# Softmax attention in a fused macaron block: the sums of the exponentials behind k's projection, the value product's third and fourth quarter in one run

## The chip, the core and the metric

The kernel runs on one NeuronCore of one Trainium2 chip, in one launch. The metric is the device time of that launch in microseconds (us), lower is better. The core has five instruction streams that work side by side and meet at semaphores: TensorE (PE, matrix products into the PSUM banks; PEld is its weight load), VectorE (DVE), ScalarE (ACT), GpSimdE (POOL) and SyncE (SP), which here only issues DMAs. Each stream is in order: an instruction that waits holds back all that stands behind it on its engine.

## The reference, cut to what matters

Eight sequences of 512 tokens with 128 channels pass six layers: a quantised feed-forward layer, softmax attention, the feed-forward layer again, a mixture of experts, a linear attention of depth 6, the mixture of experts again. The change lies in the softmax attention, with 16 heads of 64 channels, computed in float32:

```python
q = split_heads(x @ Wq.T); k = split_heads(x @ Wk.T); v = split_heads(x @ Wv.T)
sim = jnp.einsum('bhid,bhjd->bhij', q, k) * scale
m = jnp.max(sim, axis=-1, keepdims=True); e = jnp.exp(sim - m)
attn = e / (jnp.sum(e, axis=-1, keepdims=True) + EPS)
out = jnp.einsum('bhij,bhjd->bhid', attn, v)
return out.transpose(0, 2, 1, 3).reshape(B, N, INNER) @ Wo.T + bo
```

## The kernel before

The attention stage works on pairs of heads: 8 sequences x 8 pairs are 64 pairs, numbered g. It is one software pipeline, written out by hand as one loop per engine over periods (here called turns) g = -2 to 66. There is no scheduler: the order of the calls in each engine's loop is the order of its instructions, and semaphores tie the loops together. What concerns one pair is spread over four turns. In turn g, the engines do the following (kt = 0 to 3 are the four quarters of 128 keys, and TensorE's loop body goes through them):

- TensorE, in each quarter: `scores_turned(g, kt)` and `less_maximum(g, kt)` (lines 1269 and 1276, the scores with keys on the partitions, less the maximum), then `scores(g + 1, kt)` (line 1248, the scores of the next pair, from which only the maxima are taken). After quarter 0 it adds q's projection of pair g + 2 and the output product of pair g - 3 (lines 1297, 1337). After quarter 1: `add_up(g - 1)` (line 1314: sums of the exponentials, four products that fill four strips of bank `sums`), and `values(g - 1, 0)`, `values(g - 1, 1)` (line 1324: exponentials times v, in float32, into the single bank `pv`). After quarter 2: k's projection of pair g + 2 and `values(g - 1, 2)`. After quarter 3: `values(g - 1, 3)`, v's projection (line 1302) and `max_turned(g + 1)` (line 1257, which turns the maxima; it shares the bank `sums`).
- ScalarE takes the exponentials of pair g (line 1166, two for each quarter), the rounded high parts of q and k of pair g + 2 (`high`, line 1152), and copies the sums of pair g - 1 to SBUF (`total_out`, line 1172).
- VectorE takes the row maxima (`neg_max`, line 1073, two reductions for each quarter), the low parts of q and k (`low`, line 1089), the diagonal of maxima (`max_rows`, line 1081), the reciprocal of the sums (`invert`, line 1096), and the division `normalise(g - 2)` (line 1103), which empties `pv`.
- GpSimdE adds the four quarters of exponentials (line 1002) and makes the low part of the output (line 989).
- SyncE spreads the reciprocals of a pair from 32 partitions per head and half over the 64 partitions of that head, with eight DMAs (line 980), after `invert` and after the `normalise` before, since both use the one tile `rinv`.

The waits that tie a pair to the next are these. `normalise(g - 2)` waits for all eight DMAs of its pair. `values(g - 1, 0)`, the first product into `pv`, waits for `normalise(g - 2)`. `scores(g + 1, kt)` waits for the maxima of the quarter before it. `max_turned(g + 1)` waits for all maxima of pair g + 1 and for `total_out(g - 1)`. `add_up(g - 1)` waits for GpSimdE's sums, for the `total_out` before and for `max_rows(g + 1)`.

Every eighth turn `add_x` (lines 1109 and 1113) adds a sequence's output to x on VectorE, and from turn 28 on `early` puts small pieces of the next stage there. The bodies of the loops:

Of the kernel before, what the change touches and what calls it, by code (L numbers as in the profile page):

```python
# [912 lines left out]
def attn_stage(nc, mem, tag, splits=(), ahead=None):  # L913
# [7 lines left out]
    with ExitStack() as ctx:  # L921
# [42 lines left out]
        live = lambda g: 0 <= g < PAIRS_ALL  # L964
        PERIODS = range(-2, PAIRS_ALL + 3)

        with nc.Block() as block:
# [53 lines left out]
            def _(dve):  # L1021
# [70 lines left out]
                def invert(g):  # L1092
                    dve.wait_ge(total_done, g + 1)
                    if g:
                        dve.wait_ge(rinv_in, 16 * R_DMAS * g)
                    nc.vector.reciprocal(packed, total).then_inc(packed_done, 1)  # L1096
# [26 lines left out]
                for g in PERIODS:  # L1123
                    if live(g + 1):
                        neg_max(g + 1, 0)
                    if live(g - 2):
                        normalise(g - 2)
                    if live(g + 2):
                        low(g + 2, 0)
                    early(g)  # L1130
                    if live(g - 3) and (g - 3) % PAIRS == PAIRS - 1:
                        add_x((g - 3) // PAIRS)
                    if live(g + 1):
                        neg_max(g + 1, 1)
                    if live(g - 1):
                        invert(g - 1)
                    if live(g + 1):
                        neg_max(g + 1, 2)
                    if live(g + 2):
                        low(g + 2, 1)  # L1140
                    if live(g + 1):
                        neg_max(g + 1, 3)
                        max_rows(g + 1)

            @block.scalar
            def _(act):
                def high(g, which):
                    act.wait_ge(qk_done, 2 * g + 1 + which)
                    if g >= RING:
                        act.wait_ge(t_done, 8 * (g - RING + 1))  # L1150
                    scale = (DH ** -0.5 / W_ATTN, 1.0 / W_ATTN)[which]
                    nc.scalar.mul(high_of[which][g % RING][:], proj[:], scale).then_inc(hi_done, 1)

                def values_in(g):
                    act.wait_ge(v_done, g + 1)
                    if g >= 2:
                        act.wait_ge(pv_done, g - 1)
                    nc.scalar.mul(vv[g % 2][:].rearrange("p t d -> p (t d)"), proj[:], 1.0 / W_ATTN).then_inc(v_out, 1)

                def exp(g, kt):  # L1160
                    if kt == 0 and g >= 2:
                        act.wait_ge(pv_done, g - 1)
                        act.wait_ge(added, 2 * (g - 1))
                    for head in range(2):
                        act.wait_ge(t_done, 8 * g + 2 * kt + head + 1)
                        nc.scalar.activation(pT[g % 2][:, head, kt, :], turned[head][:], ACT.Exp).then_inc(exp_done, 1)  # L1166

                def total_out(g):
                    act.wait_ge(sums_done, g + 1)
                    if g:  # L1170
                        act.wait_ge(packed_done, g)
                    nc.scalar.activation(total, sums[:, 0:HALF], ACT.Copy, bias=SM_EPS).then_inc(total_done, 1)  # L1172

                def split(k, phase):
                    src, hi, lo, scale = splits[k]
                    if phase == 0:
                        if k == 0:
                            act.wait_ge(mem["moe_w_loaded"], 16 * 4)
                        nc.scalar.mul(src, src, scale).then_inc(w_scaled, 1)
                    else:  # L1180
                        act.wait_ge(w_scaled, k + 1)
                        nc.scalar.copy(hi, src).then_inc(w_hi, 1)

                def early(g):
                    b = EARLY_AT.get(g + 2)
                    if b is not None:
                        if b == 0:
                            act.wait_ge(early_known, 1)
                        else:
                            act.wait_ge(early_ratio_done, b)  # L1190
                        for t in range(TPB):
                            c = b * TPB + t
                            done = nc.scalar.activation(early_xn[:, t, :], mem["x"][:, c, :], ACT.Identity, bias=early_shift[:, c:c + 1])
                        done.then_inc(early_centred, 1)
                    b = EARLY_AT.get(g + 1)
                    if b is not None:
                        act.wait_ge(early_centred, b + 1)
                        for t in range(TPB):
                            c = b * TPB + t
                            done = nc.scalar.activation(early_xn[:, t, :], early_xn[:, t, :], ACT.Identity, scale=early_ln["rstd"][:, c:c + 1])  # L1200
                        done.then_inc(early_xn_done, 1)
                    b = EARLY_AT.get(g - 3)
                    if b is not None:
                        act.wait_ge(early_ratio_done, b + 1)
                        if b:
                            act.wait_ge(early_xg_done, b)
                        nc.scalar.activation(early_square[:], early_ratio, ACT.Square, scale=CURVE).then_inc(early_square_done, 1)

                def o_high(g):
                    act.wait_ge(o_done, g + 1)  # L1210
                    if g >= 2:
                        act.wait_ge(out_done, g - 1)
                    nc.scalar.copy(o16[g % 2][:, 0, :], oT[g % 2][:]).then_inc(o_hi, 1)

                for g in PERIODS:
                    if live(g):
                        exp(g, 0)
                    if live(g + 2):
                        high(g + 2, 0)
                    if live(g - 2):  # L1220
                        o_high(g - 2)
                    if live(g):
                        exp(g, 1)
                    if live(g - 1):
                        total_out(g - 1)
                    if 0 <= g < 2 * len(splits):
                        split(*divmod(g, 2))
                    early(g)
                    if live(g):
                        exp(g, 2)  # L1230
                    if live(g + 2):
                        high(g + 2, 1)
                    if live(g):
                        exp(g, 3)
                        values_in(g)

            @block.tensor
            def _(pe):
# [104 lines left out]
                for g in PERIODS:  # L1343
                    for kt in range(TPB):
                        if live(g):
                            scores_turned(g, kt)
                            if kt:
                                less_maximum(g, kt)
                        if live(g + 1):
                            scores(g + 1, kt)  # L1350
                        if kt == 0:
                            if live(g):
                                less_maximum(g, 0)
                            if live(g + 2):
                                project(g + 2, 0)
                            if live(g - 3):
                                output(g - 3)
                        elif kt == 1 and live(g - 1):
                            add_up(g - 1)
                            values(g - 1, 0)  # L1360
                            values(g - 1, 1)
                        elif kt == 2:
                            if live(g + 2):
                                project(g + 2, 1)
                            if live(g - 1):
                                values(g - 1, 2)
                        elif kt == 3:
                            if live(g - 1):
                                values(g - 1, 3)
                            if live(g):  # L1370
                                project(g, 2)
                            if live(g + 1):
                                max_turned(g + 1)
# [770 lines left out]
```

## Time and profile before

| What | Value |
|---|---|
| Runs | 1844.03, 1845.36, 1847.65 us; median 1845.36 |
| Profiled execution | 1844.77 us; its span 1842.6 us |
| PE busy | 1502.9 us (82%), PEld 843.7 us (46%) |
| DVE busy | 1384.0 us (75%) |
| POOL busy | 1100.4 us (60%) |
| ACT busy | 971.0 us (53%) |
| Granted TensorE clock | 0.905 of full speed over the span |

The span is the time from the first to the last instruction of one profiled execution, and all durations below are from it. Shares over the whole span mix nine stages with different limits. The attention stage runs from about 185 to 995 us of the span and is the longest; the page's line of fortieths shows PE at nine tenths all through it, at full clock. Its 64 pairs repeat one pattern, so a turn's length times 64 is nearly the stage.

The page's groups give the costs of one instruction in this stage: an exponential 594 ns (line 1166), a row maximum 684 ns (line 1073), the reciprocal 1743 ns (line 1096), an addition on POOL 1270 ns (line 1002), and a DMA of the reciprocals 1.8 us from issue to landing (line 980).

### The profile page before, as it was taken

The page shows a single profiled execution, that of the slowest core. Times are in us where ns is not written, and L with a number is a line of the kernel's source. Part 1 is how long each engine was busy: PE and PEld are TensorE (multiplying, and loading weights), DVE is VectorE, ACT ScalarE, POOL GpSimd, SP SyncE. Part 2 cuts the span into 40 slices and gives each one's busy share as a digit, 9 for nine tenths or more (in the row PEclk, how much of TensorE's full clock was granted, in tenths as well). Part 3 has the DMA queues.
Part 4 walks back from the last instruction along what each step waited for, and adds up shares of the span by engine and source line. Part 5 has one row for each costly group of instructions (what it writes and reads, how often), then busy time and mean ns, then how long its engine had stood idle before and what let it go on. Part 6 is the DMA issues. An engine that isn't in the chain of part 4 may idle for free. (4 is left out here: it accounts for less than half of the span.)

```text
span 1842.6 us, 32753 instructions
## 1 busy us (share of the span) xinstructions
PE 1502.9 (82%) x10611; PEld 843.7 (46%) x10611; DVE 1384.0 (75%) x2959; ACT 971.0 (53%) x2327; POOL 1100.4 (60%) x1434
## 2 busy tenths in 40 slices
PE   2776899999999999999996775069749999840896
PEld 1554233333333333333333555047438888740573
DVE  7997677778788878887773988358578888771683
ACT  2544466566555655555553543047328888620672
POOL 1231477877776767777773244747436666757473
PEclk9896899999999999999998887579879999955898
DMA  7000000000000000000000000233400000012335
GB/s 224 1 1 1 9 21 24 24 21 21 24 24 20 24 24 24 22 21 24 24 22 14 1 0 31 73 83 107 135 3 2 2 2 2 1 41 74 89 109 163
DMA packets 90181, 70.54 MB, mean 38 GB/s; under 512 B 16608, under 2 KB 84640, under 8 KB 90016
## 3 DMA queue, kind: packets, MB, share of 16 engines
q1 hardware_dynamic: 81312, 49.57, 10.0%
q0 software_dynamic: 8704, 18.89, 2.9%
q8 instruction: 89, 1.46, 0.3%
q14 instruction: 76, 0.62, 0.1%
HBM read 29.32 MB, written 22.30 MB: 28 GB/s over the span
## 5 line engine op out<-in xcount | busy, mean ns | idle before, releaser
L1166 ACT ACTIVATE at_pT<-at_turned 128x512 f32<-128x512 f32 x512 | 278.0, 594 | 262.4 <-PE at_turned L1276 262.4
L1073 DVE TENSOR_REDUCE at_nmax<-at_score 128x1 f32<-128x512 f32 x512 | 328.8, 684 | 111.2 <-PE at_score L1248 110.5
L1002 POOL TENSOR_TENSOR m_rows<-m_rows,at_pT 128x512 f32<-128x512 f32 x256 | 319.6, 1270 | 58.7 <-ACT at_pT L1166 58.7
L1324 PE MATMUL at_pv<-at_pT,at_v 128*64 128x512 f32 x1024 | 261.6, 611 | 0.9 <-DVE at_oT L1103 0.9
L1497 POOL DMA_INDIRECT by_token<-m_ysb,m_dest x144 | 137.9, 957 | 86.3 <-DVE m_ysb L1555 52.1
L1002 POOL TENSOR_TENSOR m_rows<-at_pT 128x512 f32<-128x512 f32 x128 | 159.7, 1267 | 46.6 <-ACT at_pT L1166 46.6
L989 POOL TENSOR_TENSOR at_o<-at_oT,at_o 128x512 f16<-128x512 f32 x64 | 77.1, 1205 | 150.3 <-issue 131.8
L1480 POOL DMA_INDIRECT by_expert<-m_rows,m_gate_slot x128 | 123.1, 962 | 60.5 <-issue 38.0
L639 POOL TENSOR_TENSOR f_hq<-f_hg,f_hsc 128x704 f32<-128x704 f32 x32 | 45.0, 1406 | 144.1 <-DVE f_hg L168 142.4
L1096 DVE RECIPROCAL m_rows<-m_rows 128x256 f32<-128x256 f32 x64 | 111.5, 1743 | 3.7 <-ACT m_rows L1172 3.6
L1297 PE MATMUL at_proj<-m_rows 128*128 128x512 f16 x384 | 108.3, 392 | 4.0 <-DVE at_own L1121 2.4
L1324 PEld LDWEIGHTS at_pv<-at_pT,at_v 128*64 128x64 f32 x1024 | 56.7, 135 | 118.2 <-issue 118.2
L1699 PE MATMUL m_x<-m_ident,m_xin 128*128 128x128 f32 x144 | 23.6, 290 | 106.2 <-DMA m_xin<-by_expert 106.2
L1710 PE MATMUL m_h<-m_w,m_x 128*128 x432 | 107.6, 386 | 3.0 <-DVE m_x L1532 3.0
L1269 PE MATMUL at_turned<-at_high_q,at_high_k 64*128 64x512 f16 x512 | 102.5, 388 | 1.0 <-ACT at_pT L1166 0.5
L1248 PE MATMUL at_score<-at_high_k,at_high_q 64*128 64x512 f16 x512 | 99.2, 381 | 3.0 <-DVE at_nmax L1073 2.3
L1269 PE MATMUL at_turned<-at_low_q,at_high_k 64*128 64x512 f16 x512 | 99.0, 378 | 0.0
L1269 PE MATMUL at_turned<-at_high_q,at_low_k 64*128 64x512 f16 x512 | 98.8, 377 | 0.0
L1276 PE MATMUL at_turned<-at_mdiag,at_unit 64*128 64x512 f16 x512 | 98.7, 377 | 0.0
L761 PE MATMUL f_gate<-m_wguT,f_xqT 128*128 128x352 f32 x128 | 63.5, 584 | 41.0 <-DVEq L570 39.5
L1269 PEld LDWEIGHTS at_turned<-at_high_q,at_high_k 64*128 64x128 f16 x512 | 25.2, 93 | 121.8 <-ACT at_pT L1166 56.6
L1636 ACT CAST m_x<-m_x 128x512 f16<-128x512 f32 x36 | 21.1, 586 | 112.7 <-PE m_x L1699 110.6
(384 smaller groups left out, 3727.4 us busy)
## 6 DMA issues: line engine op xcount, KB each, us to landing
m_rows<-m_rows SPq DMA_DIRECT2D x512, 32.0 KB, 1.8
m_xin<-by_expert SPq DMA_DIRECT2D x144, 72.0 KB
m_rows<-by_token SPq DMA_DIRECT2D x32, 256.0 KB, 4.8
by_token<-m_ysb,m_dest POOLq DMA_INDIRECT x144, 2.3
m_x<-in_x SPq DMA_DIRECT2D x8, 256.0 KB, 4.9
by_expert<-m_rows,m_gate_slot POOLq DMA_INDIRECT x128, 2.3
out_x<-m_x SPq DMA_DIRECT2D x8, 256.0 KB, 4.0
by_expert<-m_pad SPq DMA_DIRECT2D x18, 72.0 KB, 1.6
```

The lines of the kernel that those rows point to most:

```text
L1002: done = nc.gpsimd.tensor_tensor(acc, before, pT[g % 2][:, head, kt, :], ALU.add)
L1073: nc.vector.tensor_reduce(nmax[:, head * DH + qt:head * DH + qt + 1], score[head][:], AX.X, ALU.max, negate=True)\
L1096: nc.vector.reciprocal(packed, total).then_inc(packed_done, 1)
L1166: nc.scalar.activation(pT[g % 2][:, head, kt, :], turned[head][:], ACT.Exp).then_inc(exp_done, 1)
L1248: nc.tensor.matmul(score[head][:], high_of[0][g % RING][rows, qt * P:(qt + 1) * P], high_of[1][g % RING][rows, :], start=True, stop=True). ...
L1269: nc.tensor.matmul(turned[head][:], k_of[1][k][rows, tile], q_of[0][k][rows, :], start=(n == 0), stop=False)
L1276: nc.tensor.matmul(turned[head][:], unit[rows, :], mdiag[rows, :, :].rearrange("p t q -> p (t q)"), start=False, stop=True).then_inc(t_don ...
L1297: last = nc.tensor.matmul(proj[:], w[:, w_part, cols], x(x_part, 0, SEQ), start=(i == 0), stop=(i == 2))
L1324: last = nc.tensor.matmul(pv[halves[head], :], vv[g % 2][:, kt, halves[head]], pT[g % 2][:, head, kt, :], start=(kt == 0), stop=(kt == TPB ...
L1480: nc.gpsimd.indirect_dma_start(dram_rows, bass.IndirectOffsetOnAxis(slot[:, k, t:t + 1], 0), rows[k][:, t, :], None).then_inc(scattered, 16)
L1497: nc.gpsimd.indirect_dma_start(mem["dram_y_all"], bass.IndirectOffsetOnAxis(dest[j // TPB % DESTS][:, j % TPB:j % TPB + 1], 0), ysb[q % YS ...
L1710: last = nc.tensor.matmul(h[j % 3][:], x16[n % 2][:, x_part, tile], mem["w12_16"][:, w_part, ds(e, 1), :].rearrange("p e h -> p (e h)"), s ...
```

## The change

Nothing is computed otherwise. Four calls change their places. On TensorE, `add_up(g - 1)` goes from quarter 1 to quarter 2, behind k's projection, and `values(g - 1, 2)` from quarter 2 to quarter 3, in front of `values(g - 1, 3)`. On ScalarE, `total_out(g - 1)` goes behind the exponentials of quarter 2 and k's high part. On VectorE, `invert(g - 1)` goes behind the maxima of quarter 2 and k's low part.

```diff
 # VectorE
                     if live(g + 1):
                         neg_max(g + 1, 1)
-                    if live(g - 1):
-                        invert(g - 1)
                     if live(g + 1):
                         neg_max(g + 1, 2)
                     if live(g + 2):
                         low(g + 2, 1)
+                    if live(g - 1):
+                        invert(g - 1)
                     if live(g + 1):
                         neg_max(g + 1, 3)
                         max_rows(g + 1)
 # ScalarE
                         exp(g, 1)
-                    if live(g - 1):
-                        total_out(g - 1)
...
                         exp(g, 2)
                     if live(g + 2):
                         high(g + 2, 1)
+                    if live(g - 1):
+                        total_out(g - 1)
                     if live(g):
                         exp(g, 3)
 # TensorE
                         elif kt == 1 and live(g - 1):
-                            add_up(g - 1)
                             values(g - 1, 0)
                             values(g - 1, 1)
                         elif kt == 2:
                             if live(g + 2):
                                 project(g + 2, 1)
                             if live(g - 1):
-                                values(g - 1, 2)
+                                add_up(g - 1)
                         elif kt == 3:
                             if live(g - 1):
+                                values(g - 1, 2)
                                 values(g - 1, 3)
```

TensorE before, from the score pair that ends quarter 1 to the end of quarter 3, without the four products ahead of each later score pair (`at_sums<-m_rows` are the sums, `at_pv` the value product, `at_proj` with 128x512 k's projection and with 128x128 x12 v's):

```order
L1248 MATMUL at_score<-at_high_k,at_high_q 128x512 x2
L1314 MATMUL at_sums<-m_rows 32x256 x4
L1324 MATMUL at_pv<-at_pT,at_v 64x512 x4
...
L1248 MATMUL at_score<-at_high_k,at_high_q 128x512 x2
L1297 MATMUL at_proj<-m_rows 128x512 x3
L1324 MATMUL at_pv<-at_pT,at_v 64x512 x2
...
L1248 MATMUL at_score<-at_high_k,at_high_q 128x512 x2
L1324 MATMUL at_pv<-at_pT,at_v 64x512 x2
L1302 MATMUL at_proj<-m_rows 128x128 x12
L1257 MATMUL at_sums<-m_ident,at_nmax 128x128
```

The same quarters in the changed kernel:

```order
L1248 MATMUL at_score<-at_high_k,at_high_q 128x512 x2
L1324 MATMUL at_pv<-at_pT,at_v 64x512 x4
...
L1248 MATMUL at_score<-at_high_k,at_high_q 128x512 x2
L1297 MATMUL at_proj<-m_rows 128x512 x3
L1314 MATMUL at_sums<-m_rows 32x256 x4
...
L1248 MATMUL at_score<-at_high_k,at_high_q 128x512 x2
L1324 MATMUL at_pv<-at_pT,at_v 64x512 x4
L1302 MATMUL at_proj<-m_rows 128x128 x12
L1257 MATMUL at_sums<-m_ident,at_nmax 128x128
```

The value product stands in two runs of four instead of runs of four, two and two, and the sums come one quarter later.

VectorE before, one turn from the division to the diagonal of maxima:

```order
L1103 TENSOR_TENSOR at_oT<-at_pv,m_rows 128x512
L1089 SCALAR_TENSOR_TENSOR at_low_q<-at_proj,at_high_q 128x512
L1073 TENSOR_REDUCE at_nmax<-at_score 128x1 x2
L1096 RECIPROCAL m_rows<-m_rows 128x256
L1073 TENSOR_REDUCE at_nmax<-at_score 128x1 x2
L1089 SCALAR_TENSOR_TENSOR at_low_k<-at_proj,at_high_k 128x512
L1073 TENSOR_REDUCE at_nmax<-at_score 128x1 x2
L1081 TENSOR_TENSOR at_mdiag<-at_sums,at_own 128x512
```

The same turn in the changed kernel:

```order
L1103 TENSOR_TENSOR at_oT<-at_pv,m_rows 128x512
L1089 SCALAR_TENSOR_TENSOR at_low_q<-at_proj,at_high_q 128x512
L1073 TENSOR_REDUCE at_nmax<-at_score 128x1 x4
L1089 SCALAR_TENSOR_TENSOR at_low_k<-at_proj,at_high_k 128x512
L1096 RECIPROCAL m_rows<-m_rows 128x256
L1073 TENSOR_REDUCE at_nmax<-at_score 128x1 x2
L1081 TENSOR_TENSOR at_mdiag<-at_sums,at_own 128x512
```

The reciprocal stands behind one pair of maxima and k's low part more than before. SyncE's code is as it was: its eight DMAs follow the reciprocal, wherever that stands.

## Rows read from the trace of the kernel before

**Rows 1.** Busy time by stretch: length, PE, PEld, DVE, ACT, POOL, clock, DMA share, GB/s.

```profile
221.00:945.00 724.00, 723.66 (x5597) 271.18 (x5593) 579.02 (x838) 421.17 (x816) 536.97 (x437) 1.00 0.09 23
```

**Rows 2.** Timeline, TensorE, one turn: start, duration, engine, line, operation, count, idle before.

```profile
911.28 0.64 PE L1314 MATMUL at_sums<-m_rows 128*32 128x256 f32 x8
...
911.85 1.94 PE L1324 MATMUL at_pv<-at_pT,at_v 128*64 128x512 f32 x8
...
913.72 0.39 PE L1269 MATMUL at_turned<-at_high_q,at_high_k 64*128 64x512 f16 x2
...
914.59 0.38 PE L1248 MATMUL at_score<-at_high_k,at_high_q 64*128 64x512 f16 x2
...
914.90 0.82 PE L1297 MATMUL at_proj<-m_rows 128*128 128x512 f16 x3
...
915.66 1.08 PE L1324 MATMUL at_pv<-at_pT,at_v 128*64 128x512 f32 x4
...
916.67 0.39 PE L1269 MATMUL at_turned<-at_high_q,at_high_k 64*128 64x512 f16 x2
...
919.54 0.28 PE L1257 MATMUL at_sums<-m_ident,at_nmax 128*128 128x128 f32 x1
...
919.75 0.39 PE L1269 MATMUL at_turned<-at_high_q,at_high_k 64*128 64x512 f16 x2
```

**Rows 3.** Timeline, VectorE beside one score pair of TensorE, same turns.

```profile
900.32 1.74 DVE L1096 RECIPROCAL m_rows<-m_rows 128x256 f32<-128x256 f32 x1
...
902.33 0.38 PE L1248 MATMUL at_score<-at_high_k,at_high_q 64*128 64x512 f16 x2
...
904.13 0.69 DVE L1089 SCALAR_TENSOR_TENSOR at_low_k<-at_proj,at_high_k 128x512 f16<-128x512 f32 x1
...
909.84 0.68 DVE L1103 TENSOR_TENSOR at_oT<-at_pv,m_rows 128x512 f32<-128x512 f32 x1
...
912.58 1.27 DVE L1073 TENSOR_REDUCE at_nmax<-at_score 128x1 f32<-128x512 f32 x2
...
917.96 1.29 DVE L1073 TENSOR_REDUCE at_nmax<-at_score 128x1 f32<-128x512 f32 x2 [0.71 <-PE at_score L1248]
...
922.10 0.68 DVE L1103 TENSOR_TENSOR at_oT<-at_pv,m_rows 128x512 f32<-128x512 f32 x1
```

**Rows 4.** Timeline, end of the stage, waits for the copies.

```profile
958.90 0.68 DVE L1103 TENSOR_TENSOR at_oT<-at_pv,m_rows 128x512 f32<-128x512 f32 x1
...
969.56 0.69 DVE L1103 TENSOR_TENSOR at_oT<-at_pv,m_rows 128x512 f32<-128x512 f32 x1 [0.79 <-DMA m_rows<-m_rows]
...
972.73 1.75 DVE L1096 RECIPROCAL m_rows<-m_rows 128x256 f32<-128x256 f32 x1 [2.48 <-ACT m_rows L1172]
...
974.51 5.54 SPq L980 DMA_DIRECT2D m_rows<-m_rows  x8
...
981.37 0.69 DVE L1103 TENSOR_TENSOR at_oT<-at_pv,m_rows 128x512 f32<-128x512 f32 x1 [6.88 <-DMA m_rows<-m_rows]
...
982.21 3.65 PE L1324 MATMUL at_pv<-at_pT,at_v 128*64 128x512 f32 x16 [0.94 <-DVE at_oT L1103]
...
983.03 1.75 DVE L1096 RECIPROCAL m_rows<-m_rows 128x256 f32<-128x256 f32 x1 [0.97 <-ACT m_rows L1172]
...
991.06 0.69 DVE L1103 TENSOR_TENSOR at_oT<-at_pv,m_rows 128x512 f32<-128x512 f32 x1 [6.28 <-DMA m_rows<-m_rows]
```

**Rows 5.** Line 980, all copies of the stage: issue time in ns, min/median/max.

```profile
L980 SPq DMA_DIRECT2D m_rows<-m_rows x512: 507/591/1712, 214.7 to 989.2; - x171
```

**Rows 6.** Stretches of two other stages, and a wait in each (columns as above).

```profile
80.00:90.00 10.00, 7.96 (x39) 5.66 (x38) 9.58 (x16) 3.89 (x6) 2.45 (x2) 0.83 0.00 0
...
85.15 1.18 PE L761 MATMUL f_gate<-m_wguT,f_xqT 128*128 128x352 f32 x2 [1.85 <-DVEq L570]
...
1100.00:1116.00 16.00, 11.45 (x74) 9.18 (x73) 15.33 (x34) 6.57 (x10) 2.87 (x3) 1.00 0.00 1
...
1112.70 0.87 PE L785 MATMUL f_turn_h<-m_ident,f_hq 128*128 128x128 f32 x6 [1.81 <-POOL f_hq L639]
```

## The prediction

> **What bounds the kernel now.** I read the page first: the attention stage is the long stretch in which TensorE (PE) is busy nine tenths. Then the table of stretches for its steady part [rows 1]: PE is busy 723.66 of 724.00 us at full clock, VectorE (DVE) 579.02. So PE's stream sets the pace of a turn, and everything else has some slack. One turn's length is read from the same instruction twice: `normalise` starts at 909.84 and 922.10 [rows 3], so a turn is 12.27 us (12.26 by these two; the neighbours repeat 12.27), and there are 64.
>
> Next I looked for the slack of what the change moves. The reciprocal (`invert`) starts at 900.32, and the division that needs it after the eight DMAs starts at 909.84 [rows 3]: 9.52 us are there for it. How many are needed is seen only where DVE really waits for the DMAs, at the end of the stage [rows 4]: reciprocal at 972.73, division at 981.37 (8.64 us); reciprocal at 983.03, division at 991.06 (8.03 us). The parts: 1.75 for the reciprocal, the rest SyncE, which issues the eight one behind the other (median 0.59 us each [rows 5], the last one lands 1.8 us after its issue by the page). The 8.64 has one slow issue in it: the eight take 5.54 us [rows 4] instead of the some 4.9 that eight medians give, and slow ones reach 1.71 us [rows 5]. I take 8.2 on average, near the 8.03, since the median issue is the rule; bounds 8.03 and 8.64. So the slack in the kernel before is 9.52 - 8.2 = 1.3 us. That is the number on which this change turns.
>
> **The change part by part.**
>
> PE. A run of four quarter-head products of the value product takes 913.72 - 911.85 = 1.87 us, one of two takes 916.67 - 915.66 = 1.01 [rows 2]. Two runs of two become one of four: 2 x 1.01 - 1.87 = 0.15 us less per turn. The sums stand between other neighbours, but in as many changes of kind as before; I cost that at nothing (bounds -0.05 and +0.1: the dearest change in these rows is that from the value product, the cheapest under 0.05). If PE stayed the bound, a turn would be 12.12 us.
>
> ACT. `total_out` stands behind k's high part. The sums now start one k projection behind the score pair of quarter 2: 914.90 - 914.59 = 0.31, plus 915.66 - 914.90 = 0.76 [rows 2], 1.07 us. They take some 0.6 (911.85 - 911.28 = 0.57 [rows 2]), and ACT needs the time until k's high part is out in any case, since k's low part starts 904.13 - 902.33 = 1.80 us after that score pair [rows 3]. The copy (0.39) then lies beside k's low part (0.69) on DVE. Cost: nothing; if that cover were gone, some 0.2 us.
>
> DVE. Its order is now: maxima of quarter 2, k's low part, reciprocal, maxima of quarter 3. Measured from the score pair of quarter 2, the low part starts at 1.80 and the reciprocal 0.65 later (0.69 less a small overlap), at 2.45. Before, the reciprocal started 902.33 - 900.32 = 2.01 before that pair [rows 3]. The pair itself comes 0.57 earlier (the sums no longer stand ahead of it). So the reciprocal moves 2.01 + 2.45 - 0.57 = 3.9 us later in the turn. The slack was 1.3, and the turn is 0.15 shorter: the spread reciprocals come 3.9 - 1.3 + 0.15 = 2.7 us too late for `normalise`.
>
> What stands behind that wait: on DVE, q's low part and the maxima of quarter 1. On PE, `values(g - 1, 0)`, since `pv` is emptied by this division, and behind it everything. So the pace is no longer PE's stream but a ring of dependencies, once round per turn:
>
> - division starts, to first value product on PE: 982.21 - 981.37 = 0.84 [rows 4];
> - value run and four scores products, to the score pair of quarter 2: 914.59 - 911.85 = 2.74 [rows 2];
> - score pair to k's low part (exponentials and high part on ACT between them): 1.80 [rows 3];
> - low part to reciprocal: 0.65;
> - reciprocal to the next division: 8.2 (8.03 to 8.64).
>
> Sum 14.23 us (14.06 to 14.67), against 12.27: +1.96 per turn. PE alone would need 12.12, so it stands idle some 2 us in each turn, in one piece, in front of the first value product.
>
> Does the maxima's chain add to it? Reciprocal at 2.45, 1.7 for it, 1.29 for two maxima, under 0.1 to PE: `max_turned` at 5.5 after the score pair. PE would be there by 0.31 + 0.76 + 0.57 + 0.87 (scores products of quarter 3, 914.59 - 913.72) + 0.31 + 1.87 + 0.68 (v's projection, by 919.54 less the end of the run before) = 5.4 [rows 2]. It waits 0.1 us, but not on the ring: between `max_turned` and the idle piece PE has 2 us to spare. The 0.71 us that DVE waited ahead of those maxima [rows 3] is used up.
>
> Sum for the stage:
> - 60 full turns x 1.96 = 117.6;
> - the first division comes 3.9 later by its reciprocal and 9.52 - 8.2 = 1.3 sooner after it: +2.6;
> - the last three turns have no projections of later pairs. Before they took 991.06 - 958.90 = 32.2 [rows 4]. In the ring they lose k's low part and some of the matmuls, by an estimate 0.8, 1.0 and 2.2 us of 14.2: 38.6, so +6.4;
> - `add_x` stands between q's low part and the maxima of quarter 1. In such a turn these maxima start 912.58 - 909.84 = 2.74 after the division [rows 3] and end 1.3 later, at 4.05; the score pair of quarter 2 wants them at 0.84 + 2.74 = 3.58. +0.5 in 7 turns: +3.5. The `early` pieces are shorter (under 1 us) and hide;
> - TensorE's clock. Idle pieces of this size bring it down in some rows and not in others: in one stretch with a wait of 1.85 us the granted clock was 0.83 over 10 us, in another with waits up to 1.81 it stayed at 1.00 [rows 6]. One fall cost there (1 - 0.83) x 10 = 1.7 us of full-speed time. The ring's usual idle piece is near that edge (12.12 of 14.23 us busy: 2.1 less the short switches that are in both), and turns with a slow issue are over it. I put 8 falls: +13.6 (bounds 0 and 60 x 1.7 = 102).
>
> Together +144. On the profiled execution's 1844.8 us that gives 1988.5; the median of the runs shown, 1845.4, is 0.6 above it, so I forecast 1989.
>
> **A page weighed against the rows.** The rows show 6.3 to 6.9 us from the end of the reciprocal to the division [rows 4]. The Trainium skill, "DMA: Bandwidth & Descriptors", section "Anatomy of one DMA — SWDGE (gpsimd) path", gives a fixed cost of about 2.0 us per DMA, and its "Rules for kernel authors" say that issued early and waited for late, this fixed cost overlaps. Whoever costs the eight copies as one overlapped group by it has 1.75 + 2.0 = 3.75 us instead of 8.2, by an estimate, finds the division in time and forecasts the gain on PE alone. The trace disagrees in one point only: the landings overlap, the issues don't.
>
> **The rivals.**
>
> (1) The copies are in time after all, and the turn stays PE's. Mechanism: the turn's start slides enough, or the eight issues run closer than in [rows 4], so that the division isn't held. Then 0.15 x 62 = 9 us less: 1836. From which point: the reciprocal to the division has to take under 8.2 - 2.7 = 5.5 us. Against it: both waits measured are over 8, and the least issue is 0.507 us [rows 5], eight of which with reciprocal and landing still make 7.6. Chance 5%.
>
> (2) The copies are in time, but the reciprocal ahead of the maxima of quarter 3 holds `max_turned` back: 5.5 against 5.4, 0.1 per turn, which eats most of the 0.15. 1842 to 1846, no difference. Same evidence against it. Chance 3%.
>
> (3) The ring holds, and the clock falls in half of the turns or more. For it: the idle piece of some 2 us is longer than the 1.85 before which the clock fell [rows 6]. Against it: PE is busy without a break for 12 us in between, where in that stretch it wasn't (7.96 of 10 us). 30 falls give 1989 - 14 + 51 = 2026, 60 give 2077. Chance 20%. The Trainium skill, "TensorE: Matmul & The Clock Gate", section "HAM oscillation — how this bites in real kernels", tells of kernels in which each wait for a DMA lets the clock fall; by it this is the case to fear, but its waits are longer than these.
>
> (4) The ring holds, but with the bound 8.03 and no falls: 60 x 1.79 + 12 = 119, 1965. I count it in the forecast's own range, 1960 to 2010, which has 72% with it.
>
> **How the numbers follow.** Forecast 72%, clock case 20%, the two cases without the ring 8%. Faster by over 0.2% (under which no difference can be told from none): rival 1, 5%. Within 0.2%: rival 2, 3%. Slower: 92%. The range takes the forecast's own and reaches over half of the clock case: 1958 to 2040.
>
> **What would show it.** In the changed kernel's trace, the division (line 1103) waits for the DMA in nearly every one of 64 turns, 2 to 3 us each; before, it did so only at the end. PE's first value product waits some 2 us for line 1103 each turn. Turns are 14.0 to 14.3 us apart. The reciprocal starts 2.4 to 2.5 us after the score pair, and 8.0 to 8.7 ahead of the division. The clock dips in single turns. It is wrong if the turns are 12.1 to 12.3 us (rivals 1, 2), if they are 14.2 but with dips throughout (3), or if the division waits for something else than the copies.

## The result

The changed kernel takes 2009.99 us (median of 4 runs, 2001.47 to 2013.23), the kernel before 1845.19 (median of 4). The ratio is 1.0887 with a 95% interval of 1.0867 to 1.0907: slower by 165 us, where 144 were forecast (1989, range 1958 to 2040). The profiled execution has a span of 2008.2 us against 1842.6.

The table of stretches over all 63 turns of the division, then over three single turns of it (columns as in [rows 1]):

```profile
223.31:1153.25 929.94, 788.79 (x5882) 302.88 (x5882) 593.75 (x863) 441.13 (x850) 559.75 (x458) 0.96 0.07 19
253.04:267.73 14.69, 12.21 (x95) 4.81 (x95) 9.24 (x13) 7.34 (x14) 9.65 (x8) 1.00 0.08 20
267.73:283.37 15.64, 13.83 (x95) 5.11 (x95) 9.24 (x13) 7.32 (x14) 8.60 (x7) 0.89 0.06 17
283.37:297.39 14.02, 12.21 (x95) 4.82 (x95) 9.24 (x13) 7.33 (x14) 9.65 (x8) 1.00 0.08 20
```

Before, PE was busy 723.66 of 724.00 us [rows 1]. Now it is busy 12.21 in a turn of 14.02. The three turns are of three kinds: one at whose end a copy was issued late (14.69), the one behind it, with a lower granted clock (15.64, clock 0.89), and a plain one (14.02).

One round of the ring, from the timeline of the changed kernel (it answers to [rows 2 to 4]):

```profile
726.42 0.69 DVE L1103 TENSOR_TENSOR at_oT<-at_pv,m_rows 128x512 f32<-128x512 f32 x1 [2.40 <-issue]
...
727.26 1.94 PE L1324 MATMUL at_pv<-at_pT,at_v 128*64 128x512 f32 x8 [1.81 <-DVE at_oT L1103]
...
730.00 0.38 PE L1248 MATMUL at_score<-at_high_k,at_high_q 64*128 64x512 f16 x2
...
731.77 0.38 ACT L1172 ACTIVATE m_rows<-at_sums 128x256 f32<-128x256 f32 x1
731.80 0.69 DVE L1089 SCALAR_TENSOR_TENSOR at_low_k<-at_proj,at_high_k 128x512 f16<-128x512 f32 x1
...
732.41 1.74 DVE L1096 RECIPROCAL m_rows<-m_rows 128x256 f32<-128x256 f32 x1
...
740.45 0.69 DVE L1103 TENSOR_TENSOR at_oT<-at_pv,m_rows 128x512 f32<-128x512 f32 x1 [2.42 <-issue]
```

The links are 0.84, 2.74, 1.80, 0.61 and 8.04: 14.03. The profile puts DVE's wait of 2.4 us down to "issue", that is to nothing it can name; that it is the copies is seen from the distance from the reciprocal, 8.02 to 8.08 in 44 of 63 turns, the one of [rows 4], where DMA is named; the other 19 are longer, by a copy that was late. The waits of the stage:

```profile
DVE at_oT L1103 <- issue: 155.7, 59, 3.7
PE at_pv L1324 <- DVE at_oT L1103: 131.2, 63, 4.8
```

PE, which waited for the division once in the whole stage before (0.94 us, [rows 4]), waits for it 63 times, 131 us in all.

### The profile page after: what moved, and what is told of

Read it like the earlier page. It is cut to its first block and busy times, and to the rows that moved or that the text cites. A ratio compares the mean times of both kernels' runs of the same rounds, so it can differ in the third digit from the quotient of the medians.

```text
span 2008.2 us, 32753 instructions
## 1 busy us (share of the span) xinstructions
PE 1529.3 (76%) x10611; PEld 859.0 (43%) x10611; DVE 1376.6 (69%) x2959; ACT 972.2 (48%) x2327; POOL 1096.4 (55%) x1434
## 5 line engine op out<-in xcount | busy, mean ns | idle before, releaser
L1324 PE MATMUL at_pv<-at_pT,at_v 128*64 128x512 f32 x1024 | 270.7, 651 | 131.2 <-DVE at_oT L1103 131.2
L1324 PEld LDWEIGHTS at_pv<-at_pT,at_v 128*64 128x64 f32 x1024 | 71.1, 143 | 264.8 <-issue 264.8
L1103 DVE TENSOR_TENSOR at_oT<-at_pv,m_rows 128x512 f32<-128x512 f32 x64 | 44.3, 692 | 177.0 <-issue 155.7
L1213 ACT CAST at_o<-at_oT 128x512 f16<-128x512 f32 x64 | 39.5, 618 | 190.4 <-DVE at_oT L1103 190.4
```

The source lines that it names most:

```text
L1324: last = nc.tensor.matmul(pv[halves[head], :], vv[g % 2][:, kt, halves[head]], pT[g % 2][:, head, kt, :], start=(kt == 0), stop=(kt == TPB ...
```

## The experiments

All are timed beside the kernel before, on the same chip. "Turn" is the distance of two divisions, "way" that from the reciprocal's start to the division that uses it, "ring" the way plus the time from a division to the next reciprocal. A "late" copy is one that took longer to issue or to land than the usual 0.59 and 1.8 us.

**One part alone: the value product's run, without the sums.** Kernel before, with

```diff
                             if live(g + 2):
                                 project(g + 2, 1)
-                            if live(g - 1):
-                                values(g - 1, 2)
                         elif kt == 3:
                             if live(g - 1):
+                                values(g - 1, 2)
                                 values(g - 1, 3)
```

> Kernel before with one part of the change alone: the value product's third quarter goes to quarter 3, in one run with the fourth; the sums, their copy and the reciprocal stay where they were. Theory (ring of division, value product, reciprocal, copies): the reciprocal stays early, so the ring (11.0 us) stays under TensorE's turn and nothing waits for the copies. One change of kind on TensorE less gives -0.15 us per turn; but quarter 2 then holds only k's projection, 1.07 us between the score pair and the next scores products, which need the second exponential of the quarter (some 1.3 us after the pair), so TensorE waits 0.2: turn 12.3 us, 1845 to 1851 us. Rival A (only TensorE's own stream counts): turn 12.12 us, 1836. Rival B (the longer run in quarter 3 is what made the changed kernel slow): well above 1850, up to 2010.

Measured: 1854.85 us (5 runs), ratio 1.0044 (1.0030 to 1.0058). That is above the 1845 to 1851 expected. Turn 12.38, way 9.62 in most turns, so no wait for copies. The cause is seen on PE, between the score pairs of quarters 2 and 3:

```profile
910.84 0.38 PE L1248 MATMUL at_score<-at_high_k,at_high_q 64*128 64x512 f16 x2
911.04 1.08 ACT L1166 ACTIVATE at_pT<-at_turned 128x512 f32<-128x512 f32 x2 [2.26 <-PE at_turned L1276]
911.15 0.82 PE L1297 MATMUL at_proj<-m_rows 128*128 128x512 f16 x3
...
912.17 0.09 PEld L1269 LDWEIGHTS at_turned<-at_high_q,at_high_k 64*128 64x128 f16 x1 [0.18 <-ACT at_pT L1166]
```

k's projection alone is too short: the second exponential ends at 912.12, and the products of the second head start at 912.17 where they could have at 911.91. 0.26 lost, 0.15 won: 12.27 + 0.11 = 12.38. The mechanism was as expected, with 0.06 us per turn more than I had. It suggests what the sums behind k's projection are good for: they fill that hole.

**The other part alone: the sums, without the run.** Changed kernel, with `values(g - 1, 2)` back in quarter 2, behind `add_up`.

> Changed kernel with the value product's third quarter put back into quarter 2, behind the sums: so the sums, their copy and the reciprocal move, and the value product does not. Theory (ring): the ring has the same links as in the changed kernel, 14.02 us without late issues; the first value product, the score pair of quarter 2 and the reciprocal keep their distances. Late issues and falls of the clock as there: 1995 to 2020 us, within 1% of the changed kernel. Rival (the run of four in quarter 3 is the cost): back to about 1845.

Measured: 1999.57 us (4 runs), ratio 1.0824 (1.0801 to 1.0847). The plain turn is 14.02 to 14.04, the way 8.03. So the move of the sums carries nearly all of the loss, and the run none that this can tell; of the 6.9 us between the two profiled spans, 3.3 stand in two of the last three turns, where the clock was lower in the changed kernel (13.24 and 13.20 us here, 14.84 and 14.90 there), and most of the rest behind the stage. Why the clock was low there in one and not in the other is not settled.

**Half of the copies left out.**

```diff
-        R_DMAS = 8
+        R_DMAS = 4
...
-                            for to in (head * DH, head * DH + QUAD):
+                            for to in (head * DH + QUAD,):
```

> Changed kernel with only four of the eight copies of the reciprocals per pair; the other four, which go to the first 32 partitions of each head, are left out, so those rows of the output are divided by old values. Theory (the eight issues in a row make the reciprocal's way back 8.03 us): four issues less take 4 x 0.63 = 2.5 us away, the way is 5.5, the ring 11.5 us, and TensorE's stream bounds again: turn 12.1 to 12.3, 1836 to 1847 us, no falls of the clock in the stage. Rival (the way back is latency of landing or of the semaphore, not the row of issues): the ring stays over 13 us, above 1930.

Measured: 1839.68 us (9 runs), ratio 0.9957 (0.9941 to 0.9973). The kernel leaves four of the eight copies out, so that half of the rows are divided by old values; it tells only what those copies cost.

```profile
728.12 1.74 DVE L1096 RECIPROCAL m_rows<-m_rows 128x256 f32<-128x256 f32 x1
...
733.66 0.68 DVE L1103 TENSOR_TENSOR at_oT<-at_pv,m_rows 128x512 f32<-128x512 f32 x1
...
740.26 1.74 DVE L1096 RECIPROCAL m_rows<-m_rows 128x256 f32<-128x256 f32 x1
...
745.80 0.68 DVE L1103 TENSOR_TENSOR at_oT<-at_pv,m_rows 128x512 f32<-128x512 f32 x1
```

The way is 5.54, the turn 12.14, and neither row has an idle time: here DVE's own order sets the 5.54, and in the last three turns, where the division does wait for the copies, the way is 5.49 to 5.51. Four copies fewer took 2.5 us from the way, and the whole loss of 165 us is gone. The way back through the copies is therefore the cause, not the order on PE or DVE as such. (That it is the issues in a row, and not the data moved, is shown by the kernel with two queues below, which makes all eight copies.) The turn of 12.14 is also what PE's order is worth when nothing else binds: 0.13 less than 12.27.

**More copies in the old order.** Kernel before, with n = 4 or n = 2 copies more per pair, waited for with the eight (`R_DMAS` 12 or 10):

```diff
+                    for i in range(n):
+                        sp.dma_start(again[i * QUAD:(i + 1) * QUAD, :], packed[0:QUAD, :]).then_inc(rinv_in, 16)
```

> Kernel before (order unchanged) with four more copies per pair, of the same size, issued by SyncE ahead of the eight into a tile of their own, and waited for with them; nothing else. Theory (ring): before, the ring is division to reciprocal 2.5 us plus 8.03 us back, 10.5 under TensorE's 12.27; four issues more (4 x 0.635) make the way 10.57 and the ring 13.1 us, so the division starts to wait in every turn: +0.8 us per turn over 62 turns, with a late issue now and then 10 us more: 1895 to 1915 us, and no falls of the clock in the stage since TensorE's idle piece is only 0.8 us. Rival (the changed order, not the way of the copies, makes the wait): no change, 1845 to 1850.

Measured: 1958.41 us (4 runs), ratio 1.0634 (1.0618 to 1.0651). The plain way is 10.57 and the plain turn 13.21, so the ring is there in the old order too. The total is 43 us above the top of what I expected. I had costed late issues at 10 us; the way exceeds 10.57 by 0.2 us or more in 31 of 63 turns, 27 us together, and `add_x` and the `early` pieces, which before were hidden, now stand on the ring: division to reciprocal is 2.64 us without one and up to 4.99 with, 23 us together. The clock fell too, against what I expected: in seven turns the granted clock is 0.87 to 0.89. But those turns have the same division to reciprocal as their like, 2.63 us in the plain ones. In this order no value product stands between the two, and the falls cost nothing that shows.

```profile
771.12 0.69 DVE L1106 TENSOR_TENSOR at_oT<-at_pv,m_rows 128x512 f32<-128x512 f32 x1 [2.41 <-issue]
...
773.76 1.75 DVE L1099 RECIPROCAL m_rows<-m_rows 128x256 f32<-128x256 f32 x1
...
784.37 0.69 DVE L1106 TENSOR_TENSOR at_oT<-at_pv,m_rows 128x512 f32<-128x512 f32 x1 [2.07 <-issue]
...
788.99 1.74 DVE L1099 RECIPROCAL m_rows<-m_rows 128x256 f32<-128x256 f32 x1
```

> The same with two more copies per pair. Theory (ring): way back 9.30 us, ring 11.8, still under TensorE's 12.27, so nothing in the full turns; the last three turns, which wait for the copies, take 1.3 us more each: 1845 to 1852 us. Rival (each copy costs its share wherever it stands): half of what four cost.

Measured: 1883.52 us (4 runs), ratio 1.0208 (1.0193 to 1.0224). The expectation failed, and the rival didn't come true either, since half of what four cost is 57 us and two cost 40. The plain ring is 2.64 + 9.30 = 11.94, under 12.27 as I had it, but the 0.3 us to spare don't cover a late copy (up to 2.0 us of way more) or an `early` piece, and the mean turn is 12.78. It isn't enough that a ring's plain length is under the bound; it has to be under it by the ring's own scatter. The 1.5 us to spare in the kernel before (9.51 less 8.03) were just that: its late copies in the full turns disappeared in them, and PE waited for a division only once, at the end of the stage [rows 4].

**TensorE kept busy in its idle piece.** Changed kernel, with 24 small products in front of `values(g - 1, 0)` (and two waits that are long fulfilled):

```diff
...
+                for _ in range(24):
+                    nc.tensor.matmul(sums[:, HALF + P:SEQ], mem["xT"][:, 0, 0:P], mem["xT"][:, 0, 0:P], start=True, stop=True)
```

> Changed kernel plus 24 small products on TensorE (128 columns, float16, into unused columns, results not read) between the score pair of quarter 1 and the first value product, that is in TensorE's idle piece of 1.9 us; they take some 1.3 us. Theory (ring, plus falls of the clock after long idle pieces): the turn without a late issue stays 14.02 us, since the ring has that time to spare; the 17 falls of the clock with 1.6 us each go away, also after late issues: about 28 us less than the changed kernel, 1980 us. Rival A (the +1.6 us after a late issue is not the clock but a queue or buffer that runs late): stays near 2010. Rival B (TensorE's stream is the bound after all): +1.3 x 62 = 80, 2090.

Measured: 2001.41 us (4 runs), ratio 1.0847 (1.0830 to 1.0863). The clock over the stage:

```profile
228.44:1146.35 917.91, 853.89 (x7370) 382.00 (x7370) 593.71 (x864) 440.86 (x850) 558.69 (x458) 0.99 0.07 19
```

0.99 instead of 0.96. The plain turn stays 14.02, with PE busy 13.66 instead of 12.21 in it, so 1.45 us more of work per turn cost nothing: rival B is out. The clock falls twice near the stage's start and then not until its last turn, and in between no late copy is followed by 1.6 us more from division to reciprocal (6.00 where the changed kernel has 7.6): rival A is out, the +1.6 was the clock. But only 9 of the expected 28 us arrived, since late copies grew from 14 to 25 us in sum, and the first division comes 5 us later. More on the late ones below.

**Three of the eight copies on ScalarE's queue.** Changed kernel, with three `dma_start` behind `exp(g, 3)` on ScalarE.

> Changed kernel with three of the eight copies issued by ScalarE, behind the exponentials of quarter 3, where its loop has room; nothing is left out. Theory (row of issues on one queue): five issues on SyncE make the way 6.12 us and the ring 12.1, as long as TensorE's own stream (12.14): no falls of the clock, turn 12.15 to 12.3 but for turns with a late issue, which now cost up to 0.7 each in 15 turns; v's copy on ScalarE comes later by up to 1.2 us, which reaches q's projection by at most 0.3. 1838 to 1860 us. Rival (copies share the DMA engines, so two queues don't shorten the way): 14.0 us per turn, 2000.

Measured: 1874.30 us (5 runs), ratio 1.0166 (1.0152 to 1.0180). The way falls to 6.13 as it should, and 136 us of the loss are gone, with all eight copies made: what counts is the row of issues on one queue. The total missed the expected 1838 to 1860. The plain turn is 12.37, over the expected 12.15 to 12.3:

```profile
652.01 2.09 ACTq L1183 DMA_DIRECT2D m_rows<-m_rows  x3
...
654.20 0.60 ACT L1161 ACTIVATE at_v<-at_proj 128x512 f32<-128x512 f32 x1 [2.58 <-PE at_proj L1317]
...
654.85 0.82 PE L1312 MATMUL at_proj<-m_rows 128*128 128x512 f16 x3 [0.17 <-ACT at_v L1161]
```

Three issues hold ScalarE 2.1 us, v's copy comes late, and q's projection waits 0.17 for it. And 16 turns with a longer way make 21 us; in most of them a copy of SyncE's took 3.0 to 3.8 us to land instead of 1.8.

**The copies that need no DMA.** Four of the eight copies stay on their own partitions. Here ScalarE does them as ordinary copies, and SyncE issues only the other four:

```diff
...
+                    for quad in range(4):
+                        rows, cols = slice(quad * QUAD, (quad + 1) * QUAD), slice(quad % 2 * HALF, (quad % 2 + 1) * HALF)
+                        done = nc.scalar.copy(rinv[rows, cols], packed[rows, :])
...
```

> Changed kernel in which the four copies that stay on their own partitions are done by ScalarE (four copies of 32x256, behind the exponentials of quarter 3) and only the four that change partitions by SyncE's DMAs; nothing is left out. Theory (row of issues): way back 5.5 us as in the kernel with four copies left out, ring 11.5 under TensorE's 12.14, 0.6 us to spare for late issues; ScalarE needs some 1.5 us more, in time for v's copy but for 0.3 us, which q's projection doesn't see: turn 12.14, 1836 to 1844 us, so faster than the kernel before by 0.1 to 0.5%. Rival (ScalarE's copies delay v's copy and with it q's projection, as its DMA issues did in the kernel with two queues, 12.37 us per turn): 1850 to 1860.

> The same way of copying in the order of the kernel before. Theory: TensorE's stream bounds at 12.27 us and the shorter way gives nothing in the full turns, only in the last three, which wait for the copies: 1838 to 1845 us. Rival (the way of the copies cost something in the kernel before as well, by late issues): 5 us less than that. If this one and the reordered one come out equal, the reordering is worth nothing even where its ring is harmless.

Measured, with 11 runs each beside 21 of the kernel before (median 1845.05): in the changed order 1842.42 us, ratio 0.9983 (0.9969 to 0.9997); in the old order 1845.34, ratio 0.9995 (0.9983 to 1.0006).

```profile
220.42:984.50 764.08, 755.05 (x5891) 293.11 (x5891) 593.61 (x864) 547.58 (x1104) 562.94 (x458) 1.00 0.05 12
```

With its ring shortened, the changed order has turns of 12.14 and a granted clock of 1.00 over the stage, and is the one version here that leaves nothing out and beats the kernel before, by 0.17% with an interval that just excludes none. In the old order the shorter way gives nothing that can be told from none. Its plain turn is even 12.34, since v's copy stands behind ScalarE's four and q's projection waits for it:

```profile
912.77 0.33 PEld L1312 LDWEIGHTS at_proj<-m_rows 128*128 128x128 f16 x3 [0.31 <-ACT at_v L1161]
```

Only its last three turns are shorter. So the reordering is worth 0.13 us in a plain turn against the kernel before, seen here only in kernels with a way of 5.5 us, and over the 63 turns only 4.4 us (764.08 against 768.5), since turns with `add_x` or an `early` piece gain less or lose.

## Why the prediction was right, and where its sizes were off

The mechanism came out as forecast: the same wait, the same ring, link by link. The total lies 21 us above the forecast. Nearly all of that are terms that came out larger: the clock (10 us), the last three turns (5), the `early` pieces (5), the late copies (4) and what lies behind the stage (3), against some 5 us that the plain ring, the first division and `add_x` came out smaller. The 8 falls of the clock were a guess within wide bounds.

- *PE's 0.15 per turn.* 0.13 measured, in the kernels with the short way.
- *The reciprocal moves 3.9 us later, 2.7 too late for the division.* DVE waits 2.4 us in a plain turn. Right. The slack before was 1.5 us (9.51 less 8.03) rather than 1.3. Eight medians of 0.59 are 4.7 us and not the 4.9 of the prediction, but a plain row of eight does take 4.95, since the issues follow each other by 0.635.
- *The ring, 14.23 with late issues (14.06 without).* 14.02 plain, and 0.22 per turn for late copies (14 us in 63 turns) where 0.17 was in the sum. Right, link by link.
- *First division +2.6.* It came at 223.31 instead of 222.57: +0.7. Its reciprocal came 2.3 us later (215.14 instead of 212.89), not 3.9.
- *Last three turns 38.6.* They took 43.8; their granted clock was 0.89, 0.87 and 0.74. With the small products of the kernel above they took 40.0, near the forecast, so most of the miss goes with the clock.
- *`add_x` +3.5, the `early` pieces hide.* `add_x` was right: 0.47 more from division to reciprocal, where no fall of the clock covers it. The `early` pieces did not hide: four turns with them have 0.47 too, one 1.56, and two with `add_x` beside them 0.6 and 0.7 more, some 5 us that the sum put at nothing.
- *Clock: 8 falls, 13.6 us.* This term was mis-sized. In 14 of the first 60 turns the granted clock is below 1.00. In 13 of them division to reciprocal takes 1.57 to 1.66 us more than the 5.99 of a plain turn (1.7 was in the sum), in one 2.41 besides `add_x` (clock 0.81), 23.5 us together. In the one of 15.64 shown above, the first value product stands at 268.58 and the score pair at 272.94, 4.36 us apart instead of 2.74.
- *All together.* The terms account for the 166 us between the two profiled executions: 63 x 14.02 - 768.5 (the same 63 turns before) = 114.8, late copies 13.9, clock 23.5, `add_x` and `early` pieces 7.6, the last three turns 1.7, the first division 0.7, and 3.4 behind the stage, which I did not trace.
- *Rival 3 (falls in half of the turns or more)* did not happen. Of the first 60 turns, 40 begin with PE's plain idle piece of 1.80 to 1.85 us, and none of them has a lower granted clock. 19 begin with a piece lengthened by a late copy, and 13 of these have it; the 14th fall is in the first turn, behind a piece of 2.05. The length alone doesn't tell which: the 13 pieces are of 2.03 to 3.08 us, the six others of 2.17 to 2.76. What I hadn't seen is that late copy and fall go together, so that one late copy is mostly paid for twice.
- *Rivals 1 and 2* needed a way under 5.5 us. The kernel with half of the copies is nearly that case (5.49 to 5.54), and gave 1839.7 where rival 1 said 1836. The condition was too strict: by the measured links, 5.99 from division to reciprocal, the ring stays under PE's 12.14 up to a way of 6.15, with the division waiting but nothing lost. No run shows that stretch without another cost in it.
- *The Trainium skill's fixed cost of about 2.0 us per DMA* ("DMA: Bandwidth & Descriptors", "Anatomy of one DMA — SWDGE (gpsimd) path"; it is given there for DMAs issued by GpSimdE): one copy issued by SyncE takes 1.8 here, but eight in a row 6.3, since the issues follow each other by 0.635 us. The experiments with 4, 5, 8, 10 and 12 issues on SyncE have ways of 5.5, 6.13, 8.03, 9.30 and 10.57: 1.75 for the reciprocal, 1.8 for the last landing, and 0.635 for each issue but the first, to 0.05 us.

## What to carry to other kernels

Before moving a step later in a software pipeline, add up the ring that it closes, from what waits for its result back to the step, with every DMA issue of it in a row; the slack is the turn less that ring, and it has to hold the ring's scatter too. A reordering that helps the busiest engine by 1% can cost 9% through such a ring. If a row of small DMAs is on it, count the issues and not only the one latency, and take out those that an engine can do in place.

## What the runs showed of the hardware

Late copies go with what reads as the loading of code: packets of 16 KB on the queue q8, "instruction", of which the stage of the changed kernel has 49. All 18 copies that took over 0.8 us to issue began 0.15 to 0.42 us after such a packet, and none of the 17 that began within 0.35 us after one was on time. (A second such queue, q14, has 30 packets of 8 KB and doesn't go with the late ones.) One such stretch, the queues' packets and the issue's landing:

```profile
q1 hardware_dynamic: 94, 0.06, 17.6%
q8 instruction: 1, 0.02, 4.5%
issues: line engine op xcount, KB each, median us to landing
m_rows<-m_rows SPq DMA_DIRECT2D x2, 32.0 KB, 2.7
```

A stretch of the same length (1.5 us) some 14 us earlier has no such packet and lands in 1.8:

```profile
q1 hardware_dynamic: 112, 0.07, 18.4%
issues: line engine op xcount, KB each, median us to landing
m_rows<-m_rows SPq DMA_DIRECT2D x3, 32.0 KB, 1.8
```

The packets come about every 19 us in the changed kernel, and 18 of its 63 turns meet one while their copies are issued. With the 24 small products per turn they come every 15 us, nearly one turn apart: from 488 to 592 us each turn has a late issue (eight of them), in others of its stretches none. In 13 of its turns the packet comes behind the last issue; there no issue is late, but the last copy takes 2.6 to 3.5 us to land instead of 1.8. That more instructions load code more often, and that an issue or a landing waits while that happens, is what these coincidences suggest; no run varied it alone.
